# One attention and feed-forward layer: the mean weight moved into the second norm's scale and offset, the step size used as result scale, 328 instead of 304 columns on GpSimd

## The reference, cut to what matters

```python
def act_quant_fake(x):
    scale = 127.0 / jnp.clip(jnp.max(jnp.abs(x), axis=-1, keepdims=True), 1e-05)
    return jnp.clip(jnp.round(x * scale), -128.0, 127.0) / scale
def weight_quant_fake(w):
    scale = 1.0 / jnp.clip(jnp.mean(jnp.abs(w)), 1e-05)
    return jnp.clip(jnp.round(w * scale), -1.0, 1.0) / scale
...
h = layernorm(x, ln1_g, ln1_b)
h = bitlinear(h, w1, b1)            # 256 -> 1024
h = jax.nn.gelu(h, approximate=False)
h = layernorm(h, ln2_g, ln2_b)      # over 1024 columns
h = bitlinear(h, w2, b2)            # 1024 -> 256
```

## Time and profile before

| what | value |
|---|---|
| median of three runs | 1009.27 us |
| profiled execution | 1009.39 us |
| its span | 1007.7 us |
| TensorE, VectorE, ScalarE, GpSimd busy | 925.2, 905.6, 931.9, 781.3 us |
| rounding on GpSimd (line 624), mean of one | 1119 ns |
| centring on ScalarE (line 1149), mean of one | 534 ns |

### The profile page before, as it was taken

How to read it: one execution, slowest core, us unless ns; L and a number is a source line. 1 busy time by engine, 2 the same in 40 slices (tenths; PEclk the granted TensorE clock), 3 DMA queues, 4 the chain that set the end, 5 groups by cost and what they waited for, 6 DMA issues and landing times.

```text
span 1007.7 us, 26189 instructions
## 1 busy us (share of the span) xinstructions
PE 925.2 (92%) x7538; PEld 569.5 (57%) x7571; DVE 905.6 (90%) x1193; ACT 931.9 (92%) x2642; POOL 781.3 (78%) x1188
## 2 busy tenths in 40 slices
PE   9999999999999999999999998888888888888886
PEld 7666666666666666666666543344444444444435
DVE  3688888888888888888888899999999999999997
ACT  5889999999999999999998799999999999999995
POOL 2467666777667666677767588999999999999996
PEclk9999999999999999999999979999999999999999
DMA  5879988777698777877696425888887878888884
GB/s 157 167 178 191 199 163 171 170 163 159 154 181 162 166 171 169 170 144 170 152 182 148 114 64 93 127 128 127 126 127 127 126 126 126 126 126 126 126 128 92
DMA packets 243888, 146.74 MB, mean 146 GB/s; under 512 B 183896, under 2 KB 201816, under 8 KB 243824
## 3 DMA queue, kind: packets, MB, share of 16 engines
q1 hardware_dynamic: 234176, 129.03, 62.9%
q0 software_dynamic: 8640, 15.73, 12.7%
q10 hardware_dynamic: 1008, 1.18, 0.3%
HBM read 71.36 MB, written 33.63 MB: 104 GB/s over the span
## 4 chain that ended last, share of the span: by engine, by line
PE 56%; POOL 21%; issue 14%; ACT 5%; DVE 3%; POOLq 1%; DMA 0%; ACTq 0%; DVEq 0%
PE banks L1462 11%; PE banks L1448 10%; POOL nq L624 8%; PE banks L1364 6%; PE banks L1419 6%; PE banks L1408 5%; POOL out L615 4%; PE banks L1439 4%; POOL g_rq L653 3%; POOL gn_high L642 3%; PE banks L1429 3%; PE banks L1397 2%; PE banks L1433 2%; POOL gn_low L642 2%; PE banks L1289 2%
## 5 line engine op out<-in xcount | busy, mean ns | idle before, releaser
L1289 PE MATMUL banks<-w_t,h_t 128*128 128x512 bf16 x472 | 125.6, 386 | 69.7 <-DVE gn_low L878 33.8
L792 DVE TRANSPOSE_TENSOR_REDUCE nm_part<-banks 128x64 f16<-128x2048 f32 x64 | 147.6, 2306 | 1.1 <-PE banks L1364 0.7
L1084 ACT ACTIVATE probs<-banks 120x512 f32<-120x512 f32 x256 | 132.2, 603 | 14.2 <-PE banks L1397 10.6
L1145 ACT ACTIVATE g_dev<-banks,g_sum 128x1024 bf16<-128x1024 f32 x128 | 143.9, 1124 | 0.0
L1139 ACT ACTIVATE banks<-banks,h_dq 128x1024 f32<-128x1024 f32 x128 | 140.2, 1095 | 2.2 <-PE banks L1294 2.0
L1322 PE MATMUL banks<-w_t,g_t 128*128 128x256 bf16 x1024 | 133.7, 274 | 2.4 <-ACT g_t L1165 2.4
L1462 PE MATMUL banks<-wo_sb,o_t 128*128 128x256 f32 x512 | 135.0, 399 | 0.7 <-DVE xr L798 0.2
L1322 PEld LDWEIGHTS banks<-w_t,g_t 128*128 128x128 f16 x1024 | 90.2, 98 | 62.4 <-issue 51.5
L1448 PE MATMUL banks<-xt,wq_c 128*128 128x256 f32 x512 | 121.5, 380 | 0.0
L1289 PEld LDWEIGHTS banks<-w_t,h_t 128*128 (+1 forms) x504 | 47.6, 98 | 120.4 <-issue 88.8
L1462 PEld LDWEIGHTS banks<-wo_sb,o_t 128*128 128x128 f32 x512 | 87.1, 190 | 36.4 <-ACT log_sum L1073 26.1
(11 more groups left out here) (177 smaller groups left out, 2515.4 us busy)
## 6 DMA issues: line engine op xcount, KB each, us to landing
x_in<-in_x SPq DMA_DIRECT2D x64, 256.0 KB, 4.8
xt<-in_x_t SPq DMA_DIRECT2D x64, 256.0 KB, 6.1
xr<-in_x SPq DMA_DIRECT2D x64, 256.0 KB, 6.4
out<-xr SPq DMA_DIRECT2D x64, 256.0 KB, 6.4
out<-h POOLq DMA_DIRECT2D x60, 256.0 KB, 5.0
ctx_t<-in_ctx_t SPq DMA_DIRECT2D x64, 128.0 KB, 5.3
r_bc<-r_rows SPq DMA_DIRECT2D x61, 128.0 KB, 4.9
w_raw<-in_w_t SPq DMA_DIRECT2D x8, 256.0 KB, 6.7
```

The source lines that it names most:

```text
L792: dve.tensor_reduce(nm_part[:, :, 0:C * RB], blocks_p, AX.X, ALU.max, negate=True, apply_transpose=True).then_inc(max_done, 1)
L1084: act.activation(probs[:, p, j, :, :], sc_p[0:KV, j, :, :], ACT.Exp, scale=SCALE).then_inc(probs_done, 1)
L1145: act.activation(g_dev[:, t, :], u_p[t], ACT.Square, scale=-float(F), bias=g_sum[:, p, t:t + 1], accum_out=g_ssq[:, p, t:t + 1]).then_inc( ...
L1289: pe.matmul(u_p[t][:, cols], h_t[:, b, t * C + c, :], w1_t[:, c, cols], start=(c == 0), stop=False, skip_group_check=True)
```

## The change

The clipped mean magnitude of w2, until now a factor of the result scale, goes into the rows ln2_g and ln2_b. During the first part SyncE loads both rows as columns, ScalarE multiplies them by the mean, SyncE stores them to a DRAM tensor `gain_rows`, and the broadcast loads before the second part read that tensor. The normed rows, their maximum, and the step size `g_vm[..., T:2T]` then carry the factor, so that the step size is also the result scale. GpSimd's `out_scale` of each batch and the buffer `g_dq` are dropped; the last batch keeps one such operation. `g_vm` gets four buffers. The three waits of `quantise_batch` become a function `quantise_waits`, called ahead of `gain_part` of tile 1 and no longer ahead of the rounding. PART becomes 328.

```diff
-    PART = 304
+    PART = 328
+    gain_rows = nc.dram_tensor("gain_rows", [2, F], F32, kind="Internal").ap()
...
+                def load_cols():
+                    load_bias()
+                    for n, src in enumerate((ln2_g, ln2_b)):
+                        sp.dma_start(gain_cols[:, n, :], src.rearrange("(p n) -> p n", p=P)).then_inc(cols_loaded, 16)
+                def store_rows():
+                    sp.wait_ge(cols_scaled, 1)
+                    sp.dma_start(gain_rows.rearrange("r (p n) -> p r n", p=P), gain_cols[:, :, :]).then_inc(rows_stored, 16)
...
                 def load_gains():
                     sp.wait_ge(x_ssq, NB * T)
-                    for dst, src in ((g2_bc, ln2_g), (b2n_bc, ln2_b)):
+                    sp.wait_ge(rows_stored, 16)
+                    for n, dst in enumerate((g2_bc, b2n_bc)):
                         sp.wait_ge(kvq_ps, NB)
-                        sp.dma_start(dst[:, :], src.rearrange("(a n) -> a n", a=1).to_broadcast([P, F])).then_inc(gains_loaded, 16)
+                        sp.dma_start(dst[:, :], gain_rows[n].rearrange("(a n) -> a n", a=1).to_broadcast([P, F])).then_inc(gains_loaded, 16)
...
-                aside = {..., W_STEP - 1: load_bias, ...}
+                aside = {..., W_STEP - 1: load_cols, NB - 6: store_rows, ...}
...
-                def out_scale(b, r):
-                    pool.tensor_tensor(g_dq[:, r, :], g_max[:, r, :], w_out[:, 0:1].to_broadcast([P, T]),
-                                       ALU.mult).then_inc(gdq_done, 1)
-
-                def quantise_batch(b, r):
+                def quantise_waits(b, r):
                     pool.wait_ge(gr_done, b + 3)
-                    if isinstance(b, int) and b == 0:
-                        pool.wait_ge(w_out_done, 1)
                     if isinstance(b, int) and b == NB - 2:
                         pool.wait_ge(gt_ps, T)
                     else:
                         for t in range(T):
                             after(pool, g_turned[r % 2][t], 8 * (b - r % 2))
-                    out_scale(b, r)
+
+                def quantise_batch(b, r):
                     for t in range(1 if isinstance(b, int) and b == NB - 3 else T):
                         quantise_rows(t, r, g_rq[:, r % 2, T + t:T + t + 1])
...
-                    scales(j, n % 2)
+                    scales(j, n)
+                    quantise_waits(j - 2, (n + 2) % 4)
                     gain_part(j, 1, n)
                     quantise_batch(j - 2, (n + 2) % 4)
...
                 last_scales()
+                quantise_waits(NB - 2, 2)
                 quantise_batch(NB - 2, 2)
...
                 pool.wait_ge(last_quant, 1)
-                out_scale(NB - 1, 3)
+                pool.tensor_scalar(last_dq[:, :], g_max[:, 3, :], 1.0 / QMAX, 0.0, ALU.mult, ALU.add).then_inc(gdq_done, 1)
...
-                    dve.tensor_scalar(w_out[:, :], w_mean[:, 1:2], 1.0 / QMAX, None, ALU.mult).then_inc(w_out_done, 1)
...
-                        dve.memset(gn_floor[n], CLIP).then_inc(floor_set, 1)
+                        dve.wait_ge(w_scaled, 1)
+                        dve.tensor_copy(gn_floor[n], w_floor[:, :].unsqueeze(1).to_broadcast([P, T, 1])).then_inc(floor_set, 1)
...
-                    after(dve, gdq_done, j - 3)
+                    after(dve, gmx_done, j - 3)
...
-                dve.wait_ge(gdq_done, NB)
+                dve.wait_ge(gmx_done, NB - 1)
...
+                def copy_mean_weight():
+                    act.wait_ge(mean_done, 1)
+                    act.activation(w_floor[:, :], w_mean[:, 1:2], ACT.Copy, scale=CLIP).then_inc(w_scaled, 1)
+                    act.wait_ge(cols_loaded, 16 * 2)
+                    act.activation(gain_cols[:, :, :], gain_cols[:, :, :], ACT.Copy, scale=w_mean[:, 1:2]).then_inc(cols_scaled, 1)
+                aside[W_STEP + 17] = copy_mean_weight
...
                 def residual(b, t, r):
-                    act.wait_ge(gdq_done, b + 1)
                     act.wait_ge(y2_ps, b * T + t + 1)
                     if t == 0:
                         after(act, stored[r], (b - r) * 4)
-                    act.activation(res[:, r, t, :], y2_tiles[t], ACT.Copy, scale=g_dq[:, r, t:t + 1]).then_inc(out_done, 1)
+                    act.activation(res[:, r, t, :], y2_tiles[t], ACT.Copy, scale=g_vm[:, (r + 2) % 4, T + t:T + t + 1]).then_inc(out_done, 1)
```

More of the change, by code:

```diff
@@ L95, in xattn_ffn @@
         w_mean = sb("w_mean", [P, 2])
-        w_out = sb("w_out", [P, 1])
         bias_mov = sb("bias_mov", [P, F], BF16)
@@ L134, in xattn_ffn @@
         mean_done = sem("mean_done")
-        w_out_done = sem("w_out_done")
         w_rounded = sem("w_rounded")
@@ L231, in xattn_ffn @@
         g_ssq = sb("g_ssq", [P, 2, T])
-        g_vm = sb("g_vm", [P, 2, 2 * T])
+        g_vm = sb("g_vm", [P, 4, 2 * T])
+        w_floor = sb("w_floor", [P, 1])
+        gain_cols = sb("gain_cols", [P, 2, F // P])
+        cols_loaded = sem("cols_loaded")
+        cols_scaled = sem("cols_scaled")
+        rows_stored = sem("rows_stored")
+        w_scaled = sem("w_scaled")
         g_rq = sb("g_rq", [P, 2, 2 * T])
@@ L237, in xattn_ffn @@
         last_inverse = sb("last_inverse", [P, T])
-        g_dq = sb("g_dq", [P, 4, T])
+        last_dq = sb("last_dq", [P, T])
         h_inv = sb("h_inv", [P, NB, T])
@@ L395, in load_gains_turn_bias @@
                     turn_bias(2, 1)
-                aside = {0: load_last, 1: load_rows, W_STEP - 1: load_bias, W_STEP + 9: store_bias, W_STEP + 13: place_bias,
+                aside = {0: load_last, 1: load_rows, W_STEP - 1: load_cols, NB - 6: store_rows, W_STEP + 9: store_bias, W_STEP + 13: place_bias,
                          NB - 2: turn_first_bias, NB - 1: load_gains_turn_bias}
@@ L646, in first_scales, with scales @@
                     pool.wait_ge(gve_done, b + 1)
-                    pool.tensor_tensor(g_rq[:, b % 2, 0:T], g_vm[:, b % 2, 0:T], powers[:, 0:T], ALU.pow).then_inc(gr_done, 1)
-                def scales(b, p):
+                    pool.tensor_tensor(g_rq[:, b % 2, 0:T], g_vm[:, b % 4, 0:T], powers[:, 0:T], ALU.pow).then_inc(gr_done, 1)
+                def scales(b, n):
                     pool.wait_ge(g_affine, (b - 1) * T)
@@ L652, in scales @@
                     pool.wait_ge(gmx_done, b - 1)
-                    pool.tensor_tensor(g_rq[:, p, :], g_vm[:, p, :], powers[:, :], ALU.pow).then_inc(gr_done, 1)
+                    pool.tensor_tensor(g_rq[:, n % 2, :], g_vm[:, n, :], powers[:, :], ALU.pow).then_inc(gr_done, 1)
                 def last_scales():
@@ L701, in _ @@
                 add_b2(NB - 1, 3)
-                scales(2, 0)
+                scales(2, 2)
+                quantise_waits(0, 0)
                 gain_part(2, 1, 2)
@@ L975, in _ @@
                 steps(dve, 4, NB, FFN_L0, FFN_L1, ffn, 4, {4: lambda: invert_scales(2)})
-                dve.wait_ge(gdq_done, NB - 4)
+                dve.wait_ge(gmx_done, NB - 4)
                 for t in range(T):
@@ L988, in _, with add_residual @@
                 dve.tensor_scalar(nq[:, 1, 1, :], gn[3][:, 1, :], last_scale[:, 1:2], HALF_ONE, ALU.mult, ALU.add).then_inc(last_quant, 1)
-                def add_residual(b, t, r, y):
-                    dve.scalar_tensor_tensor(out=xr[:, r, t, :], in0=y[t], scalar=g_dq[:, r, t:t + 1],
+                def add_residual(b, t, r, y, scale):
+                    dve.scalar_tensor_tensor(out=xr[:, r, t, :], in0=y[t], scalar=scale[:, t:t + 1],
                                              in1=xr[:, r, t, :], op0=ALU.mult, op1=ALU.add).then_inc(last_out, 1)
@@ L995, in _ @@
                 dve.wait_ge(x1_stored[2], NB * 4)
-                dve.wait_ge(gdq_done, NB)
+                dve.wait_ge(gmx_done, NB - 1)
                 for t in range(T):
                     dve.wait_ge(y2_ps, (NB - 2) * T + t + 1)
-                    add_residual(NB - 2, t, 2, y2_first)
+                    add_residual(NB - 2, t, 2, y2_first, g_vm[:, 0, T:2 * T])
                 dve.wait_ge(x1_stored[3], NB * 4)
+                dve.wait_ge(gdq_done, 1)
                 for t in range(T):
                     dve.wait_ge(last_y, t + 1)
-                    add_residual(NB - 1, t, 3, y2_tiles)
+                    add_residual(NB - 1, t, 3, y2_tiles, last_dq)
             @block.scalar
@@ L1150, in deviation, with variance @@
                                    bias=g_nm[:, p, t:t + 1]).then_inc(part_centred, 1)
-                def variance(b, p):
+                def variance(b, p, n):
                     after(act, gr_done, b - 1)
                     act.wait_ge(ssq_done, b * T + T)
-                    act.activation(g_vm[:, p, 0:T], g_ssq[:, p, :], ACT.Copy, scale=1.0 / F ** 3, bias=LN_EPS).then_inc(gve_done, 1)
+                    act.activation(g_vm[:, n, 0:T], g_ssq[:, p, :], ACT.Copy, scale=1.0 / F ** 3, bias=LN_EPS).then_inc(gve_done, 1)
                 def step_size(b, r):
@@ L1159, in step_size @@
                     act.wait_ge(g_maxed, b + 1)
```

(4 more changed lines are left out.)

## The result

The changed kernel takes 1017.62 us (median of four runs, 1017.11 to 1018.68), the kernel before 1009.77 in the four runs that stand beside it. The medians are 7.9 us apart. The ratio measured over the runs is 1.0072, with a 95% interval of 1.0059 to 1.0084, which is 7.3 us slower, 6.0 to 8.5. The profiled execution took 1017.11 us with a span of 1015.4; that of before had a span of 1007.7.

What follows compares the result with a forecast made beforehand. GpSimd, at 6.43 us a batch against 6.336 now, was to become the engine that sets the pace: 1009.4 + 4.9 in the loop - 0.2 in the tail = 1014.1 us, range 1006.8 to 1017.5.

Steps and rivals of the forecast that it cites:

- The moved wait: GpSimd's loop: product of tile 1 waits for the power instruction, gap 0.16 or some 0.29 against -0.01, +0.24 us a batch.
- Columns: GpSimd's two products a batch: 24 more columns each at 2.2 ns a column, +0.10 us a batch.
- `out_scale`: GpSimd between product and rounding: the scale instruction goes, 0.92 against 1.07 us, -0.15 a batch.
- rival A: GpSimd stays hidden at 6.22 or below, ScalarE sets the pace with 6.32; 1008.4 us in total, chance 0.31.
- Sum of the loop: GpSimd's batch: 6.24 + 0.10 - 0.15 + 0.24 = 6.43 us against 6.336, +4.9 us over 52 batches.
- The floor's copy: VectorE: setting the floor by a copy instead of a memset happens four times and costs nothing.
- First part: ScalarE's two instructions, three small DMAs and a SyncE wait: hidden by ScalarE's spare 2.5 us; uncovered, 0.3 once.
- TensorE's slack: TensorE's 2.0 us between a rounded tile's landing and use lasts some 20 batches, to near 770 us; then it waits.
- VectorE idle 0.15 a batch: Sign of the forecast: VectorE stands idle some 0.15 us a batch late in the loop.
- The tail: End of the kernel: `out_scale` goes ahead of the rounding of batch 62, which TensorE awaits, -0.2 us.
- Rival B: GpSimd hidden, ScalarE regains what the columns cost, VectorE's 6.28 sets the pace; 1005.9 us, chance 0.12.

Runs made afterwards that it cites:

- e1: Changed kernel with GpSimd's wait for its own power instruction put back behind the product of tile 1; 1011.67 us.
- e2: Kernel before, with only the three waits moved ahead of the product of tile 1 on GpSimd; 1019.02 us.
- e3: Kernel before, with 328 columns on GpSimd instead of 304, its scale instruction and order of waits kept; 1010.37 us.
- e10: Changed kernel with the floor of the first four batches set by a memset of the constant 1e-5 instead of a copy; 1017.13 us.
- e9: Kernel before, with the floor of the first four batches copied from a column instead of set by a memset; 1011.06 us.
- e7: Changed kernel with the power instruction's wait back behind the product and the floor set by a memset of the constant; 1011.56 us.
- e5: Changed kernel with the wait for the power instruction last of the three waits, still ahead of the product of tile 1; 1019.20 us.

## Why the prediction was nearly right

The direction and the mechanism were right, and the number was 3.5 us too low. The median is 0.1 above the upper end of the range. In the profiled execution the loop took 1.5 more than forecast, the part ahead of it 2.05 where nothing was forecast, the end 0.6 less, and the median lies 0.5 above that execution. Step by step:

- **The moved wait** was the cause, as forecast: e1 takes it back and the loop is at 6.340, e2 adds it alone and has 6.501. The size was 0.24 and measures 0.27 (0.26 against -0.01). The failing part of that step is "about three where it must be made" with "a gap of 0.16 and of some 0.29": the odd batches have the 0.16, the even ones 0.30 and 0.41. The number of instructions behind the release was right, one and three; the price of three was too low.
- **Columns** +0.10 on GpSimd: the product went from 0.82 to 0.88, twice 0.05 to 0.06; in e3 they alone added 0.018 a batch in spacing and nothing in the median.
- **`out_scale`** -0.15: product to rounding 0.98 against a forecast of 0.97. The 0.10 between product and rounding stayed, so rival A had no ground.
- **Sum of the loop**: 6.43 forecast, 6.459 measured; 52 times the 0.03 is the 1.5 us.
- **The floor's copy** was costed at nothing because it is four short instructions. Its cost was not its own work but the instruction of GpSimd that it meets. In the profiles it is 0.7 us of the changed kernel's 2.05 (e10).
- **First part**, forecast 0: the span from one transposing reduction of VectorE to the fifth next is 43.74 us in before, e2, e3 and e9 (560.36 - 516.62 and its like, 43.73 to 43.74), and 43.93 to 43.95 in the six kernels that store the scaled rows from SyncE at step 58. The changed kernel, with that store:

```profile
516.99 2.31 DVE L804 TRANSPOSE_TENSOR_REDUCE nm_part<-banks 128x64 f16<-128x2048 f32 x1
525.99 2.31 DVE L804 TRANSPOSE_TENSOR_REDUCE nm_part<-banks 128x64 f16<-128x2048 f32 x1
...
560.93 2.30 DVE L804 TRANSPOSE_TENSOR_REDUCE nm_part<-banks 128x64 f16<-128x2048 f32 x1
```

```profile
527.67 0.43 SPq L373 DMA_DIRECT2D gain_rows<-gain_cols  x1
```

  The 0.2 us is there at the first step already, 9.00 us against 8.75 before (525.37 - 516.62), and that is ahead of the store's row. So it isn't the store's own transfer; what else these six kernels have in common there is open. Another 0.4 was there at 517 us (516.99 against 516.62). Its source is open too: e3, which changes nothing in the first part, has 516.93, and e9 516.50.
- **Between 561 and 584 us** the changed kernel's profile loses 0.6 more, ahead of any copy. A transposing DMA on SyncE was recorded 2.85 us long, before 1.60 and 1.12 in e1, and the load of `xr` behind it was issued at 576.32 instead of 574.51. GpSimd's addition waited for that load:

```profile
580.52 1.27 POOL L570 TENSOR_TENSOR xr<-xr,bo_bc 128x512 f32<-128x512 f32 x1 [1.88 <-DMA xr<-in_x]
```

  Before, the same addition starts at 579.26 and waits for VectorE. Since e1 has the same first part and its addition starts at 579.91, this belongs in part to the one execution. With 0.4, 0.2, 0.6 and the 0.7 of the copies 1.9 of the 2.05 have a place, and only the last a cause that a run isolates.
- **TensorE's slack** of 2.0 us, used up near 770: the lag of the power instruction behind ScalarE's variance is 0.5 at 655 us, 1.5 at 707 and 2.2 from about 740 on, where it stays. The size held to 0.2, and the place came some 30 us early, as a loop that loses more asks for.
- **VectorE idle 0.15 a batch**: by the spacing it is 6.459 - 6.28 = 0.18. Little of it shows as waits (2.2 us in the 200 from 740); the rest are late starts. From reduction to the next centring it is 2.36 in the mean over that stretch, 2.20 before, which makes 0.15.
- **The tail**, -0.2: from the store of batch 60 to the last power instruction it is 1000.55 - 977.49 = 23.06 us, before 992.68 - 969.00 = 23.68. e1 and e7, which drop the scale instruction as well, have 23.53 and 23.52, so the forecast fits them; the 0.5 more in the changed kernel was not followed up.

```profile
1000.55 0.69 POOL L667 TENSOR_TENSOR g_rq<-g_vm,powers 128x2 f32<-128x2 f32 x1
```

Rival A is what e1 and e7 are: with the old order back, GpSimd is hidden and ScalarE sets 6.34. Rival B asked for 6.28, and neither came near it. Dropping an instruction from GpSimd could gain nothing, since GpSimd was waiting for ScalarE in every batch already, and e7, the best version of the change that was run, is not faster than the kernel before (1.0004 to 1.0025). Whether fewer columns, 304 or 316, would let it fall below 6.336 was written down as a question; no time was measured for either.

## What to carry to other kernels

A wait for the engine's own previous instruction is a real wait: put an independent instruction between the two, and price moving it by every queue instruction left between the release and the next start. Count these in the queue and not in the source (e5). A recorded start before the recorded end of the instruction ahead is no gain by itself; compare ends. Before a small operation changes its kind (memset to copy), look at what the neighbour engine runs beside it. Removing work from an engine which only waits for another one brings nothing; look at who releases it first.

## What the runs showed of the hardware that was not expected

- GpSimd behind its own instruction: 0.14 with one semaphore instruction in between, 0.16 with one register instruction, 0.25 with two instructions, 0.30 or 0.41 with three. Without a wait the next one starts 0.01 to 0.33 before the recorded end, and ends 0.85 to 0.86 behind it either way (e1, e3).
- A power instruction that starts 0.67 to 0.69 behind a store lasts 1.31 to 1.33 us; one that waits for ScalarE and starts 1.07 behind it lasts 1.03. Their ends lie 2.0 and 2.1 behind the store: an early recorded start is not an early end.
- A copy of 128x2 values on VectorE lasted 0.15 to 1.29 us, and in the changed kernel three of four ended within 0.03 of the end of an instruction of GpSimd's; a memset of the same lasted 0.06.
- 24 more columns on ScalarE cost what was forecast, 0.02 a copy (807.79 - 807.37 = 0.42 in the changed kernel against 0.40 in the earlier trace rows), and yet e1 with 328 runs at 6.340 and before with 304 at 6.336. The 0.08 that ScalarE waited at the other copy took it up: from that copy to the gelu it is 0.46 in the mean before and 0.43 in e1, from 740 to 940 us.
